# Router logits: tokens on the partitions by short matmuls, in place of logits turned back by transposes

## What is computed

```python
# ffn0: dense part, and 8 experts of which 2 are chosen per token
xr = _rms(x) * router_scale * ROOT
probs = softmax(xr @ router_w)              # router_w: 256 x 8
top_w, top_i = top_k(probs, 2)
# ffn1: 8 experts of which 4 are chosen per token
gate = xt @ wg                              # wg: 256 x 8
top_val, top_idx = top_k(gate, 4)
gs = softmax(top_val)
out = einsum('nk,nko->no', 1 + gs - gs, take(einsum(relu(xt @ w1), w2), top_idx))
```

## Time and profile before

| | us |
|---|---|
| median of 3 runs (lowest, highest) | 506.76 (504.17, 507.1) |
| the profiled execution, its time | 502.75 |
| the profiled execution, its span | 500.8 |
| TensorE busy in the span | 459.9 (92%) |
| TensorE's weight loads | 394.1 (79%) |
| VectorE busy | 363.4 (73%) |
| ScalarE busy | 270.7 (54%) |

### The profile page before, as it was taken

How to read it: one execution, slowest core, us unless ns; L and a number is a source line. 1 busy time by engine, 2 the same in 40 slices (tenths; PEclk the granted TensorE clock), 3 DMA queues, 4 the chain that set the end, 5 groups by cost and what they waited for, 6 DMA issues and landing times. The chain is left out here.

```text
span 500.8 us, 9620 instructions
## 1 busy us (share of the span) xinstructions
PE 459.9 (92%) x3062; PEld 394.1 (79%) x3062; DVE 363.4 (73%) x1196; ACT 270.7 (54%) x599; POOL 155.9 (31%) x221
## 2 busy tenths in 40 slices
PE   1999999999999999999999887999689998799996
PEld 1788888899888898887988766888568777678885
DVE  4668798768456887367885488898398878359685
ACT  3657643455544855445755486364547666644531
POOL 2001000341007710046410436358014334325352
PEclk9999999999999999999999999999899999899999
DMA  6333350033223342142434312671777220000101
GB/s 204 113 93 95 92 193 1 33 116 99 82 88 103 106 131 81 50 146 80 138 89 136 116 41 96 73 112 27 260 202 247 72 65 1 1 2 2 42 1 42
DMA packets 35328, 45.96 MB, mean 92 GB/s; under 512 B 4401, under 2 KB 27825, under 8 KB 35281
## 3 DMA queue, kind: packets, MB, share of 16 engines
q1 hardware_dynamic: 31920, 38.55, 27.0%
q0 software_dynamic: 2304, 6.29, 4.0%
q10 hardware_dynamic: 1056, 0.52, 0.4%
HBM read 26.47 MB, written 16.25 MB: 85 GB/s over the span
## 5 line engine op out<-in xcount | busy, mean ns | idle before, releaser
L793 PE MATMUL ps<-zh,w0u_h 128*128 128x512 f32 x160 | 65.2, 407 | 1.8 <-ACT zh L1394 1.5
L794 PE MATMUL ps<-zh,w0u_l 128*128 128x512 f32 x160 | 63.4, 396 | 0.0
L795 PE MATMUL ps<-zl,w0u_h 128*128 128x512 f32 x160 | 63.3, 396 | 0.0
L2236 DVE SCALAR_TENSOR_TENSOR x<-ps,aff,x 128x256 f32<-128x256 f32 x128 | 53.0, 476 | 10.0 <-PE ps L795 8.3
L793 PE MATMUL ps<-w0d_h,ah 128*128 128x256 f32 (+1 forms) x205 | 58.1, 284 | 0.4 <-DVE al L1902 0.2
L795 PE MATMUL ps<-w0d_l,ah 128*128 128x256 f32 (+1 forms) x205 | 57.2, 279 | 0.0
L794 PE MATMUL ps<-w0d_h,al 128*128 128x256 f32 (+1 forms) x205 | 57.1, 279 | 0.0
L697 POOL TENSOR_TENSOR al<-act,ah 128x512 fp32r<-128x512 f32 x27 | 35.0, 1295 | 45.5 <-ACT ah L1558 43.9
L2319 DVE CUSTOM_DVE_ANT_0 ps<-ps,bias 128x256 f32<-128x256 f32 (+1 forms) x128 | 42.4, 384 | 7.5 <-PE ps L1234 6.6
L711 POOL TENSOR_SCALAR_AFFINE_SELECT pbt<-pbt 128x256 f32<-128x256 f32 x64 | 25.9, 409 | 59.9 <-ACT pbt L1688 59.5
L1423 ACT ACTIVATE gel<-ps 128x512 f32<-128x512 f32 x40 | 23.9, 598 | 36.1 <-PE ps L795 36.0
(11 more groups left out here) (240 smaller groups left out, 1354.9 us busy)
## 6 DMA issues: line engine op xcount, KB each, us to landing
stage<-in_w_dram SPq DMA_DIRECT2D x16, 384.0 KB, 3.1
stage<-z_rows SPq DMA_DIRECT2D x21, 256.0 KB, 2.9
y_rows<-tmp SPq DMA_DIRECT2D x21, 256.0 KB, 2.1
qs<-split_out SPq DMA_DIRECT2D x24, 128.0 KB, 2.6
ks<-split_out SPq DMA_DIRECT2D x48, 64.0 KB, 2.4
stage<-in_w_dram SPq DMA_DIRECT2D x8, 256.0 KB, 3.0
z_rows<-tmp SPq DMA_DIRECT2D x1, 1920.0 KB, 8.3
ks<-pad SPq DMA_DIRECT2D x6, 256.0 KB, 9.3
```

Of the source, the lines that this page charges most:

```text
L793: pe.matmul(o, lh, rh, start=start, stop=False, **kw)
L794: pe.matmul(o, ll, rh, start=False, stop=False, **kw)
L795: return pe.matmul(o, lh, rl, start=False, stop=stop, **kw)
L2236: i = V.scalar_tensor_tensor(xt, ps[:, base + t // 2, (t % 2) * D:(t % 2 + 1) * D], aff[:, b, t, e:e + 1], xt, ALU.mult, ALU.add)
```

## The change

The logits are made in one step with the tokens on the partitions. Stationary are now the activations (`zh` or `zl` of one chunk and one tile of 128 tokens), moving are the 8 columns of the router weights. That is 4 tiles x 2 chunks x 3 = 24 matmuls, each with a weight load of 128 x 128 and 8 moving columns, and they write the 128 x 32 logits directly. The copy by ScalarE, its two semaphores and the four transposes are gone, as are the zero columns of the weights, the two memsets that GpSimd made for them and VectorE's wait for those memsets. At sites 0 and 4 to 7 the matmuls write to the same bank in which the turned-back logits ended before (6 or 3); at sites 1 to 3 this is bank 3 where the turned logits went to bank 2. All 24 stand where `logits_t` stood.

```diff
-        wr_h = sb("wr_h", [P, 2, KC, P], F32R)
-        wr_l = sb("wr_l", [P, 2, KC, P], F32R)
+        wr_h = sb("wr_h", [P, 2, KC, E], F32R)
+        wr_l = sb("wr_l", [P, 2, KC, E], F32R)
...
-        lgt = small[0:E, :]
...
-            nc.gpsimd.memset(wr_h[:, :, :, :].bitcast(F32), 0.0).then_inc(setup_pool, 1)
-            nc.gpsimd.memset(wr_l[:, :, :, :].bitcast(F32), 0.0).then_inc(setup_pool, 1)
...
-            def logits_t(which, bank, first):
-                if first:
-                    pe.wait_ge(wr_split, 1)
-                for kc in range(KC):
-                    mm = split3(ps[:, bank, :], wr_h[:, which, kc, :], wr_l[:, which, kc, :],
-                                zh[:, kc, :], zl[:, kc, :], kc == 0, kc == KC - 1)
-                mm.then_inc(lgt_ps_s, 1)
-
-            def logits(bank, n):
-                pe.wait_ge(lgt_s, n + 1)
+            def logits(which, bank):
+
                 for t in range(BT):
-                    mm = pe.transpose(ps[:, bank, t * E:(t + 1) * E], lgt[:, t * P:(t + 1) * P], ident[0:E, 0:E])
+                    for kc in range(KC):
+                        mm = split3(ps[:, bank, t * E:(t + 1) * E], zh[:, kc, t * P:(t + 1) * P], zl[:, kc, t * P:(t + 1) * P],
+                                    wr_h[:, which, kc, :], wr_l[:, which, kc, :], kc == 0, kc == KC - 1)
                 mm.then_inc(lg_ps_s, 1)
...
                 n = units(st, b, "ffn0")
-                which, bank = (0, 2) if st.kind == "ffn0" else (1, 3)
                 down0(n - LAG)
                 split_ready(norm(st, b))
                 pe.wait_ge(prod_s, n)
-                logits_t(which, bank, False)
+                logits(int(st.kind == "ffn1"), 3)
                 down0(n - 1)
-                logits(3, routed[st.kind, st.k + b])
...
                     if c == 1:
-                        logits_t(0, 6, True)
+                        pe.wait_ge(wr_split, 1)
+                        logits(0, 6)
...
-                    if c == 3:
-                        logits(6, routed["ffn0", 0])
...
                             if before(st, b) != "ffn0":
-                                logits_t(1, 3, not f0)
+                                logits(1, 3)
...
-                        if c == 1 and not first_later(n):
-                            logits(3, routed["ffn1", fb])
...
-            def logits_t_out(n, bank):
-                act.wait_ge(lgt_ps_s, n + 1)
-                nc.scalar.activation(lgt, ps[0:E, bank, :], ACT.Copy).then_inc(lgt_s, 1)
...
-                dve.wait_ge(setup_pool, 3)
...
-                V.tensor_copy(wr_h[:, :, :, 0:E], wr_raw[:, :, :, :]).then_inc(step, 1)
+                V.tensor_copy(wr_h[:, :, :, :], wr_raw[:, :, :, :]).then_inc(step, 1)
                 dve.wait_ge(step, 1 + KC)
-                V.tensor_tensor(wr_l[:, :, :, 0:E], wr_raw[:, :, :, :], wr_h[:, :, :, 0:E].bitcast(F32),
+                V.tensor_tensor(wr_l[:, :, :, :], wr_raw[:, :, :, :], wr_h[:, :, :, :].bitcast(F32),
                                 ALU.subtract).then_inc(wr_split, 1)
```

More of the change, by code:

```diff
@@ L243, in program @@
         down1_s = sem("down1_ready")
-        lgt_ps_s = sem("logits_t_in_psum")
-        lgt_s = sem("logits_t_ready")
         lg_ps_s = sem("logits_in_psum")
@@ L1489, in dense_block @@
                         act_hi(c - 1)
-                    if c == 2:
-                        logits_t_out(routed["ffn0", 0], 6)
                     gelu(c)
@@ L1506, in routed_block @@
                         left_hi(st, b)
-                        logits_t_out(routed["ffn0", fb], 2)
                         if fb > 1:
@@ L1564, in first_block @@
                 left_hi(st, 0)
-                logits_t_out(routed["ffn1", 0], 3)
                 dense_squares(last)
@@ L1597, in ffn1 @@
                                 out_hi(3, 1)
-                            logits_t_out(routed["ffn1", fb], 3)
                         if c == 0 and before(st, b) == "attn1":
```

## The result

| | before | after |
|---|---|---|
| median (lowest, highest), us, 6 runs each | 505.28 (504.17, 507.1) | 523.2 (520.39, 524.88) |
| the profiled execution, its time | 502.75 | 524.43 |
| its span | 500.8 | 522.5 |
| mean granted clock | 0.991 | 0.958 |

The account below looks back on a forecast made before the run. TensorE's own instruction stream was taken to bound most of the span. Sites 0 to 3 (2.84), 4 (1.24), 5 (1.24), 6 and 7 (0.80) sum to 6.1 us, giving 512.9 us by the 506.76 median; range 507.5 to 516.5.

Parts of the forecast that it names:

- Price of a load: New logits matmuls: one float32r load follows another after 0.11 us, so the stretch of 24 takes 2.72 us.
- Quick loads: Rival, new logits stretch: loads before short matmuls are cheaper, 0.07 or 0.025 us per pair, sum -1.5 or -10.1 us; 12%.
- TensorE's own lengthening: All eight sites: TensorE's longer logits stretch, less the transposes, adds 6.1 us in sum.
- Sites 0 to 3: TensorE runs nearly without a gap there, so each site costs the full 0.71 us: 2.84 us.
- Site 4: The last down product ends 1.24 us later, and ScalarE's squares and the whole chain move with it: +1.24 us.
- Site 5: VectorE's left accumulation starts 1.24 us later, the chain to TensorE's wait has no slack: +1.24 us.
- taken up behind: Rival, behind sites 1 to 3: TensorE's idle time absorbs what they add, sum +4.0 us, 510.8; 15%.
- Sites 6 and 7: The exponential delays VectorE's mask product some 0.4 us, TensorE's wait absorbs the rest: +0.40 us each, 0.80 together.
- The clock falls: Rival, new stretches: few moving columns drop TensorE's clock to 0.50, up to 1.7 us per fall, 519.7 to 526.5; 13%.
- The base: Whole kernel: the forecast starts from the shown runs' median, 506.76 us, not the profiled execution's 502.75.

Follow-up runs that it names:

- e9: The kernel before, unchanged, profiled again on the chip of the experiments; 505.8 us, ratio 1.0001.
- e12: e1 with GpSimd waiting at site 4, ahead of the fifth of its eight gathers, for the last down product; 512.39 us, ratio 1.0117.
- e1: The changed kernel with its 24 short matmuls per site padded to 128 moving columns, 120 of them zeros; 515.12 us, ratio 1.0204.
- e14: The kernel before with only GpSimd's wait for the last down product at site 4 added; 506.35 us, ratio 1.0003.
- e15: The changed kernel (8 moving columns) with GpSimd's wait for the last down product at site 4 added; 520.9 us, ratio 1.0292.
- e6: e1 with ScalarE's wait, a copy of constants nobody uses and TensorE's wait for it kept; 517.88 us, ratio 1.0218.
- e7: The kernel before with the new logits of 8 columns at sites 0, 5, 6 and 7 only; 514.75 us, ratio 1.016.
- e13: e8 with GpSimd waiting at site 4, within its row of gathers, for the last down product; 505.21 us, ratio 0.9983.
- e3: The changed kernel with its 24 matmuls of 8 columns laid between long ones; 526.38 us, ratio 1.0383.
- e4: e3 with high and low router weights side by side (16 and 8 moving columns), so 16 loads per site; 512.99 us, ratio 1.0155.
- e8: The changed kernel with high and low router weights side by side, padded to 128 moving columns, 16 loads per site; 507.41 us, ratio 1.0028.

## Why the prediction was wrong, step by step

The distance from one site's first logits matmul to the next one's, in five of the profiles (us):

| | before | e9, before again | e12 | e1 | after |
|---|---|---|---|---|---|
| start to 0 | 20.59 | 19.88 | 20.19 | 20.34 | 20.76 |
| 0 to 1 | 64.05 | 63.99 | 64.65 | 64.65 | 64.63 |
| 1 to 2 | 69.02 | 69.04 | 69.92 | 69.83 | 73.04 |
| 2 to 3 | 69.02 | 70.45 | 70.79 | 70.56 | 71.47 |
| 3 to 4 | 62.01 | 63.40 | 64.14 | 65.44 | 65.11 |
| 4 to 5 | 31.54 | 31.90 | 32.89 | 35.99 | 35.92 |
| 5 to 6 | 126.31 | 126.66 | 126.51 | 126.44 | 128.85 |
| 6 to 7 | 28.32 | 28.29 | 29.00 | 29.02 | 32.13 |
| 7 to end | 29.94 | 29.89 | 30.61 | 30.63 | 30.59 |
| span | 500.8 | 503.5 | 508.7 | 512.9 | 522.5 |

- **Price of a load: right.** 0.112, and 2.68 for the stretch. The Trainium skill's 81 ns per pair ("TensorE: Matmul & The Clock Gate", "Back-to-back issue gap") does not hold for these loads; its section "LDWEIGHTS (loading the stationary operand)", columns / 1.2, gives an estimate of 107 ns for 128 columns, and the distance of 112 ns in the trace is near it (each load lasts 190 ns by its own record). Quick loads are out.
- **TensorE's own lengthening: near in sum, in part by luck.** e12 has full clock at the sites and no late increment at site 4. Against e9 its span is 5.2 us longer (6.1 forecast), of which 0.3 lie ahead of site 0 and are none of the change. Sites 0 to 3 cost 0.66, 0.88, 0.34 and 0.74, in sum 2.6 (2.84 forecast). Site 4 costs 0.99 (1.24), though this piece is 31.54, 31.90 and 32.74 in before, e9 and e14, with the old logits in all three. The sum is near because site 5 came out too high and sites 6 and 7 too low.
- **Site 5: too high, the wait that ends last was another.** VectorE's left accumulation did start 1.3 later against the site's start, as the 1.24 said (5.71 in e12, 4.41 in e9). But the down product of TensorE that waits for the first accumulation came only 0.77 later (15.65, 14.88), with the same 0.37 of idle time as before, not 0.9. Between them stands VectorE's product with the mask, beside a subtraction of GpSimd. In e9, then in e12:

```profile
328.97 1.30 POOL L697 TENSOR_TENSOR al<-act,ah 128x512 fp32r<-128x512 f32 x1 [2.07 <-ACT ah L1558]
329.50 0.82 DVE L1833 TENSOR_TENSOR em<-lex,selm 128x32 f32<-128x32 f32 x1
```

```profile
333.66 1.30 POOL L694 TENSOR_TENSOR al<-act,ah 128x512 fp32r<-128x512 f32 x1 [1.52 <-ACT ah L1539]
334.73 0.28 DVE L1812 TENSOR_TENSOR em<-lex,selm 128x32 f32<-128x32 f32 x1
```

  Both times it ends 0.05 behind GpSimd's instruction, which TensorE feeds by way of ScalarE and which moved by 0.77. By site 6 0.2 is left, against the first profile, whose low clock in this part is as long as e12's. The attention stage between took that up: that was my rival "taken up behind", in one place.
- **Sites 6 and 7: too low, for the same reason.** 0.71 and 0.72, not 0.40. At site 7 VectorE's product with the mask starts 0.38 later, as I had it. But it does not end 0.2 behind its start. In e9, then in e12, with GpSimd's subtraction beside it:

```profile
481.07 1.30 POOL L697 TENSOR_TENSOR al<-act,ah 128x512 fp32r<-128x512 f32 x1 [0.66 <-ACT ah L1558]
481.43 0.99 DVE L1833 TENSOR_TENSOR em<-lex,selm 128x32 f32<-128x32 f32 x1
```

```profile
484.86 2.65 POOL L694 TENSOR_TENSOR al<-act,ah 128x512 fp32r<-128x512 f32 x2
486.29 1.27 DVE L1812 TENSOR_TENSOR em<-lex,selm 128x32 f32<-128x32 f32 x1 [2.89 <-ACT lex L1395]
```

  It ends 0.05 behind GpSimd's instruction both times (482.42 and 482.37; 487.56 and 487.51), though it is work of 0.18 (its time at sites 0 to 4). GpSimd's subtraction is fed by TensorE and moved with its 0.7, and so the chain did. I had read the 0.98 in the earlier trace rows and not asked what it was. The Trainium skill names this ("SBUF — State Buffer", "SBUF: two separate sides"): an operation of VectorE with two SBUF inputs and one of GpSimd that reads SBUF exclude each other for a whole instruction. The rows agree.
- **"The clock falls": this is the step that failed.** I gave it 13%, and against it that TensorE's loads stand back to back and that a stretch with 2.04 of 4.00 us busy had kept 1.00. The sum had the clock at nothing. e1 beside after, and e12 beside e15, show that loads back to back do not hold it when 8 columns move behind each: 6.3 to 9.6 us, by which measure and pair one takes. Of the 9.6 us of span between e1 and after, 3.2 lie between sites 1 and 2, 0.9 between 2 and 3 and 3.1 between 6 and 7, behind stretches of low clock of 6.8, 3.4 and 6.8 us. At site 4 the fall is hidden (35.99 and 35.92), since TensorE waits there anyway, and behind site 3 it does not show in the distance either. The 2.4 between 5 and 6 are not the short matmuls' by any run: they go with a low clock from 386.9 to 393.8, in the attention stage 56 us behind site 5. e9 has such a stretch too (374.9 to 381.7), and e6, with 128 columns, needs 128.82 there like after. The rival's price, up to 1.7 per fall of 3.4 us, was fair. That its times (519.7 to 526.5) hold the 523.2 is in part luck, as some 3 us of that are the late increment at site 4; but e15, without it, is at 520.9. The rival deserved most of the chance, as a row of busy time said nothing on what a short matmul does.
- **Site 4, the late increment: the second term that was at nothing.** From e12 to e1 the piece from site 4 to 5 grows by 3.1 us, and from e15 to after by 2.8. I had watched which product the squares wait for, and not what else ran at that time. The piece from 3 to 4 grows by 1.3 from e12 to e1, but up to there the two kernels do the same work, and this piece differs between profiles of one text too (62.01 in before, 63.40 in e9). So the 1.3 are put down to the execution and not to the late increment at site 4.
- **The base: right.** By the median, 505 to 507, not by the profiled 502.75. e9 says why: the first profile of before lacks 2.7 us that e9's has, and none of the timed runs of before is under 503.5.

The parts add up by the spans: 5.2 (e9 to e12: TensorE's work) + 3.1 (late increment at site 4) + 1.1 (the rest of e12 to e1, not the change's) + 7.2 (e1 to after without the piece from 5 to 6: for the most part clock at the sites) + 2.4 (that piece: low clock, not shown to be the change's) = 19.0 = 522.5 - 503.5. These are single profiles, so each part is good to about a microsecond.

## What to carry to other kernels

Before a wide moving operand is traded for many loads with a few moving columns, price the clock beside the loads: pad the moving operand once and compare, since here 128 columns cost nothing beside a load. When a product that another engine waits for moves by a microsecond, look at what it moves into, on the other queues too. And profile the kernel before a second time before a difference of single waits is put down to a change, and look in a control's own trace whether it does what it is the control of.

## What was not expected of the hardware

- Loads of 128 x 128 back to back with 8 columns behind each let the granted clock fall to 0.50: 45.6 us of low clock, 51.3 with the same matmuls spread between long ones, against 12.8 with 128 columns. It doesn't fall at every site in every profile: sites 1, 2, 3, 4 and 6 in after, sites 0, 5 and 7 in e7. Far from the sites it differs too: between sites 5 and 6 the low clock is 6.8 us in before, 10.2 in e9 and none in e13.
- TensorE's semaphore increments can come up to 3.2 us late (295.15 to 298.34 in e1) beside a row of GpSimd's indirect DMAs, often 1.2 us behind the last of the row, while TensorE's matmuls run on. Away from such rows the logits' increments stand 0.01 behind the matmul's end. At sites 2 and 3 the logits' increment was late in every profile but the first one of before, by 1.95 to 2.65 us, but in e3 and e4, where the logits end later against the row, by 0.2 to 1.5. At site 4 the logits' or the down product's was late by 0.6 us or more in all kernels with the new logits there but e3, e12, e13 and e15. That the one at site 4 is tied to the row is shown by e12 and e15. The end of the row is not the whole rule: in e8 the product's increment came at 290.82, while the last gather ran until 292.52. What holds the increments, and why those in the earlier part of a row mostly come at once, is open.
- VectorE's product of two SBUF inputs, work of 0.18 us, lasted up to 1.27 us (e12, site 7) and ended 0.05 behind GpSimd's subtraction each time.
